# A one-core transformer block with routed experts: when the pre-split expert words are reloaded, and when the first block of rows is turned

## The chip, the cores and the metric

The kernel runs on one core of one Trainium2 chip. The metric is the device time of one execution in microseconds (us). The kernel before has a median of 651.16 us over three runs (649.86 to 651.72).

## The reference, cut to what matters

```python
x = L0_attn_x                                  # [2, 1024, 256], f32
mod = (silu(L0_c) @ L0_wmod).reshape(2, 6, 1, 256)
sa, ca, ga, sb, cb, gb = (mod[:, i] for i in range(6))       # ga, gb kept away from zero
h = layernorm(x) * (1 + ca) + sa
x = x + ga * attention(h)                      # 16 heads of 16, causal softmax, biases
h = layernorm(x) * (1 + cb) + sb
xt = h.reshape(2048, 256)
cw = combine_weights(xt, gate_w)               # 16 experts, best 2 of 4 groups, top 4, normalised
for e in range(16):
    out += cw[:, e:e+1] * (swiglu(xt @ expert_up_w[e].T) @ expert_down_w[e].T)
out += swiglu(xt @ shared_up_w.T) @ shared_down_w.T
return x + gb * out
```

The change touches only the way from the shared expert (the last line but one) to the sixteen routed experts (the loop).

## The kernel before, in words

**Stages.** Attention runs first (eight groups of heads, `attention(body)`). Behind it comes the shared expert: 20 steps in the order of `S_ORDER` (line 287), of which "u" steps make the up products of one chunk of 512 tokens and one slice of features, and "d" steps the down products; the last two, steps 18 and 19, are `("d", 3, 0)` and `("d", 3, 1)`. Last come the routed experts. The 2048 tokens times 4 choices are sorted by expert into 79 blocks (`NB`) of 128 rows, each block with a single expert; a block's expert has a number no higher than the block's. After the blocks the expert outputs are read back, scaled and summed.

**Words.** All products are made as three products of high and low parts ("split words"). An item k of the 18 (`NW`) is half of the shared expert (k = 0, 1) or one expert (k = 2 to 17). Items up to 10 are loaded raw and split on ScalarE (`high_words`) and VectorE (`low_words`) during the shared expert. Items 11 to 17 (`PRE` is 11) are split by GpSimd during attention and stored in HBM as `expert_words`; they come back, ready, by `load_final` (line 883; its transfer is issued on line 887), 1088 KB each. I call these seven transfers F11 to F17. `place_free` (line 835 on) makes a final wait until its place in SBUF is free: F11 and F12 wait among others until the last chosen rows are in HBM (line 849), F14 to F17 until the shared expert's last down products are made (`s_down`, line 842).

**The order of the transfers.** All these transfers are issued by SyncE (SP) in program order on one queue. `POST_SP` (line 241) says what SP issues after each step of the shared expert, `BLOCK_SP` (line 306) what it issues behind the rows of a block. The SP loop of the blocks is

```python
for b in range(NB):
    load_block(b)
    for piece in BLOCK_SP.get(b, ()):
        work(piece)
```

`load_block(b)` (line 952 on) reads the blocks' addresses from a small table, four at a time (line 957), and issues the load of the block's 128 rows, 132 KB, into one of four buffers `G` (line 977). I call it Gb. Before it issues, block 0 waits for all chosen rows and the pads; a block from 4 on waits for the block four before it to have been turned and its output rows found (lines 973, 974; YIX on line 1942); and

```python
if PRE <= b + NSH < NW:
    sp.wait_ge(w_raw[b + NSH], WORDS_IN)
```

with `NSH` = 2: the load of block b = 9 to 15 waits on SP until the final b + 2 has landed.

**A block on the engines.** TensorE turns its rows (`turn_unit`, lines 2362 to 2370, two transposes; tb below is the time at which block b's start), ScalarE takes the high part of the turned rows (`turn_high`, line 1418), VectorE the low part and the row numbers of the outputs (`turn_low`, lines 1929 to 1942), then TensorE makes the up products (`up_unit`, line 2415), ScalarE and VectorE the activation (lines 1424, 1968), TensorE turns it (line 2427) and makes the down products (lines 2439 to 2444), ScalarE copies the result out and GpSimd scatters it to HBM (line 1233). The turn of block s + 2 stands in TensorE's program behind the up products of block s. `turn_unit(u)` waits for Gu and for `turn_low(u - 1)`.

**At the seam.** In both engine programs `turn_unit(0)` and `turn_low(0)` stand behind step `SN - 2` = 18, so before the last step of the shared expert, whose down products (`s_down_tiles(3, 1)`, line 2335), four idle products (`idle_products`, line 2381, all at 128 x 512) and whose sum on VectorE (`s_add(3, 1)`, lines 1923 and 1927) come after them. Block 1's turn stands behind those.

Of the kernel before, what the change touches and what calls it, by code (L numbers as in the profile page):

```python
# [117 lines left out]
def interleave():  # L118
# [121 lines left out]
EARLY_LOADS = {6: (3, 4, 5), 7: (6,)}  # L240
POST_SP = {
    -1: [("store", 2), ("load", 7)], 2: [("turned", 2)], 6: [("store", 3)], 7: [("turned", 3)], 9: [("load", 8), ("load", 9)],
    11: [("pads", 0, 16)], 12: [("load", 10), ("final", 11), ("final", 12)],
}

LAST_OUT = 5
# [45 lines left out]
SN = len(S_ORDER)  # L292
# [10 lines left out]
assert all(PLACE[NSH + e] == NSH + e + sum(d for first, d in PLACE_STEPS if e >= first) for e in range(NE))  # L303
BLOCK_DVE = {1: [("lo", 10)]}

BLOCK_SP = {3: [("final", 13), ("final", 14)], 5: [("final", 15)], 6: [("final", 16)], 8: [("final", 17)]}
for _table, _lead in ((BLOCK_DVE, 5), (BLOCK_SP, 3)):
    assert all(_s <= _p[1] - _lead for _s in _table for _p in _table[_s])

# [20 lines left out]
def program(nc, x, wqk, bqk, wv, bv, wout, bout, cT, wmod, wgate, wsh, wexp, qkd, modrows, hTd, xd, padd, zd, wd, out):  # L330
    with ExitStack() as ctx:

        def sem(name):
            return ctx.enter_context(nc.semaphore(name))
# [279 lines left out]
        pads = sem("pads")  # L614
# [148 lines left out]
        def _(sp):  # L763
# [188 lines left out]
            def load_block(b):  # L952
                if b == 0:
                    sp.wait_ge(tab_ready, 1)
                if b % SP_LOAD == 0:
                    n = min(SP_LOAD, NB - b)
                    _, values = nc.values_load_multi_w_load_instructions(
                        rbt[0:1, b:b + n], engines=(mybir.EngineType.SP,), min_val=0, max_val=XROWS // P - 1,
                        skip_runtime_bounds_check_because="a block lies in its expert's stretch or behind all of them")
                    where.update({b + k: v for k, v in enumerate(values)})  # L960
                if b == 0:
                    for c in range(NC):
                        sp.wait_ge(xs_out[c], 16 * TPC * TOPK)
                    sp.wait_ge(pad_out, 16 * NE)

                    for k in range(PRE, NW):
                        sp.wait_ge(w_raw[k], WORDS_OUT)
                if b >= GRING:

                    sp.wait_ge(t1_ps, b - GRING + 1)  # L970
                    sp.wait_ge(yix_step, 2 * (b - GRING) + 2)


                sp.wait_ge(w_lo, NSH + min(b, PRE - NSH - 1) + 1)
                if PRE <= b + NSH < NW:
                    sp.wait_ge(w_raw[b + NSH], WORDS_IN)
                sp.dma_start(G[b % GRING][:, :], xd.rearrange("(n p) w -> n p w", p=P)[bass.ds(where[b], 1)].rearrange(
                    "a p w -> p (a w)")).then_inc(g_in[b % GRING], 16)

            def work(piece):  # L980
                if piece[0] == "store":
                    store_turned(piece[1])
                if piece[0] == "turned":
                    load_turned(piece[1])
                if piece[0] == "pads":
                    pad_experts(sp, mybir.EngineType.SP, piece[1], piece[2])
                if piece[0] == "load":
                    load_words(piece[1])
                if piece[0] == "final":
                    load_final(piece[1])  # L990
# [4 lines left out]
# [4 lines that stand above are left out]
# [476 lines left out]
        def _(dve):  # L1475
# [35 lines left out]
            def row_maximum(n, u):  # L1511

                i, diag, _, w = ROWS[u // HG]
                j = u % HG
                dve.wait_ge(m_ps, n * UNITS + (u + 1))
                dst = mxA[:, i, j:j + 1] if diag else mxB[:, i - TPC, j:j + 1]
                nc.vector.tensor_reduce(dst, mbank[u % RING][:, 0:w], AX.X, ALU.max).then_inc(m_red, 1)  # L1517
# [318 lines left out]
            def work(piece):  # L1836
                what = piece[0]
                if what == "res":
                    residual(piece[1], piece[2])
                if what == "stats":  # L1840
                    statistics(piece[1], piece[2])
                if what == "aggr":
                    averages(piece[1], piece[2])
                if what == "rows":
                    make_rows(piece[1], piece[2])
                if what == "soft":
                    soften(piece[1])
                if what == "ta":
                    copy_out(piece[1], piece[2])
                if what == "route":  # L1850
                    route(piece[1], piece[2], piece[3])
                if what == "norm":
                    normalise(piece[1])
                if what == "tot":
                    totals()
                if what == "tab":
                    block_tables()
                if what == "lo":
                    low_words(dve, nc.vector, piece[1])
                if what == "xl":  # L1860
                    rows_low(piece[1])
# [39 lines left out]
            def s_multiply(c, f):  # L1901
                i, n = FC * c + f, FEATS[f]
                dve.wait_ge(s_silu, i + 1)
                if i >= 2:
                    dve.wait_ge(s_low, i - 1)
                nc.vector.tensor_tensor(s_act[i % 2][0:n, :], s_up[i % 2][1][0:n, :], s_gate[i % 2][0:n, :],
                                        ALU.mult).then_inc(s_mult, 1)

            def s_rest(c, f):
                i, n = FC * c + f, FEATS[f]  # L1910
                dve.wait_ge(s_high, i + 1)
                nc.vector.tensor_tensor(s_al[i % AHR][0:n, :], s_act[i % 2][0:n, :], s_ah[i % AHR][0:n, :].bitcast(F32),
                                        ALU.subtract).then_inc(s_low, 1)

            def s_add(c, i):

                n, y = 2 * c + i, Yall[:, 2 * i:2 * i + 2, :]
                dve.wait_ge(s_down, n + 1)
                if n == 0:
                    dve.wait_ge(modrow_in, 48)  # L1920
                if n >= 2:
                    dve.wait_ge(x_add, n - 1)
                nc.vector.tensor_tensor(y, s_out[i].rearrange("p (t h) -> p t h", t=2), GBr[:, c // (S // CH), :].unsqueeze(1)
                                        .broadcast_to([P, 2, H]), ALU.mult).then_inc(s_gated, 1)
                dve.wait_ge(s_gated, n + 1)
                t = X[:, 2 * n:2 * n + 2, :]
                nc.vector.tensor_tensor(t, t, y, ALU.add).then_inc(x_add, 1)

            def turn_low(u):
                dve.wait_ge(xh_done, u + 1)  # L1930
                nc.vector.tensor_tensor(xl[u % 2][:, :], xbank[:, 0:H], xh[u % 2][:, :].bitcast(F32),  # L1931
                                        ALU.subtract).then_inc(xl_done, 1)
                find_outputs(u)
# [10 lines left out]
            for s in range(-1, SN):  # L1944
                if s >= 0 and S_ORDER[s][0] == "u":
                    s_multiply(*S_ORDER[s][1:])
                for piece in POST_DVE.get(s, ()):
                    work(piece)
                if s >= 0 and S_ORDER[s][0] == "u":
                    s_rest(*S_ORDER[s][1:])  # L1950
                if s >= 0 and S_ORDER[s][0] == "d" and not any(s in late for late in LATE_SUMS.values()):
                    s_add(*S_ORDER[s][1:])
                for d in LATE_SUMS.get(s, ()):
                    s_add(*S_ORDER[d][1:])
                for piece in POST_DVE.get(s + 0.5, ()):
                    work(piece)
                if s == SN - 2:

                    turn_low(0)

# [59 lines left out]
        def _(pe):  # L2020
# [351 lines left out]
            def idle_products(s):  # L2372

                if s < 2:
                    pe.wait_ge(s_mult, 1)
                    to = s_up[0][0]
                else:
                    was_read(pe, ("cnt",))
                    to = allb[0]
                for i in range(IDLE_PE[s]):  # L2380
                    nc.tensor.matmul(to[:, :], Wsh[:, 0:P], Wsh[:, P:P + CH], start=True, stop=True)

            for s in range(-1, SN):
                if s >= 0:
                    (s_multiply if S_ORDER[s][0] == "u" else s_down_tiles)(*S_ORDER[s][1:])
                if s in IDLE_PE:
                    idle_products(s)
                for piece in POST_PE.get(s, ()):
                    work(piece)
                if s == SN - 2:  # L2390
                    turn_unit(0)

            expert = {}
# [134 lines left out]
```

## Time and profile before

| | us |
|---|---|
| median of three runs | 651.16 (649.86 to 651.72) |
| span of the profiled execution | 644.6 |
| rest of the median that lies outside such a span | 6.6 |
| TensorE busy | 582.1 (90%) |
| VectorE busy | 487.5 (76%) |
| ScalarE busy | 382.8 (59%) |
| GpSimd busy | 337.9 (52%) |

The profiled execution has no time of its own on record beside its span; the 6.6 us is the median less the span. Times of the trace are counted from the start of the span. SPq is SyncE's own instruction stream (it issues transfers), PEld TensorE's weight load. In a row of the chain or timeline the first number is the start, the second the duration; a bracket at the end is how long the engine had been idle before the row and what ended that.

### The profile page before, as it was taken

How to read it: one execution, taken by the hardware profiler on the slowest of the kernel's cores; microseconds unless marked ns; L12 is line 12 of the kernel's file. 1: busy time of each engine (PE TensorE's matmuls, PEld its weight loads, DVE VectorE, ACT ScalarE, POOL GpSimd, SP SyncE). 2: the span in 40 equal slices, each digit the busy share in tenths (PEclk: the TensorE clock that was granted, in tenths of full speed). 3: DMA queues.
4: the chain of work that ended last, by engine and by line, in shares of the span. 5: the costliest groups of instructions: out<-in, count | busy, mean ns of one | idle time of the engine just before them, and what ended most of it. 6: DMA issues, size and time to landing. Idle time of an engine off the chain costs nothing. (4 is left out here: it accounts for less than half of the span.)

```text
span 644.6 us, 13664 instructions
## 1 busy us (share of the span) xinstructions
PE 582.1 (90%) x3960; PEld 395.7 (61%) x3960; DVE 487.5 (76%) x1415; ACT 382.8 (59%) x926; POOL 337.9 (52%) x585
## 2 busy tenths in 40 slices
PE   3879879999999999998997799997799999999996
PEld 3657533434343444444342378776799999999985
DVE  4888978888888868776967568898566766666648
ACT  3546437666766656655858552643356777776662
POOL 5524614455747527763738876774144444444430
PEclk9989969999999999998999989999799999999999
DMA  8349965961707273451305243665964444444498
GB/s 270 137 158 288 334 221 151 243 210 71 216 26 224 87 209 141 136 185 63 118 34 174 77 150 115 232 217 207 364 220 134 135 135 134 133 135 134 126 374 335
DMA packets 69066, 113.62 MB, mean 176 GB/s; under 512 B 12578, under 2 KB 51106, under 8 KB 67844
## 3 DMA queue, kind: packets, MB, share of 16 engines
q1 hardware_dynamic: 62036, 93.74, 45.3%
q0 software_dynamic: 6864, 19.01, 7.6%
q8 instruction: 34, 0.56, 0.4%
q14 instruction: 36, 0.29, 0.1%
q10 hardware_dynamic: 96, 0.01, 0.0%
HBM read 60.57 MB, written 49.94 MB: 171 GB/s over the span
## 5 line engine op out<-in xcount | busy, mean ns | idle before, releaser
L1377 ACT ACTIVATE Pr<-bank 128x512 f32<-128x512 f32 (+3 forms) x384 | 165.5, 494 | 94.8 <-PE bank L2166 91.1
L1517 DVE TENSOR_REDUCE mxA<-bank 128x1 f32<-128x128 f32 (+3 forms) x256 | 112.2, 484 | 23.9 <-PE bank L2062 23.7
L1233 POOL DMA_INDIRECT expert_rows<-Y,YIX x79 | 75.7, 959 | 104.0 <-DVE ytmp L1938 75.5
L2166 PE MATMUL bank<-Qs,Ks 99*128 99x512 bf16 (+3 forms) x384 | 118.6, 332 | 8.0 <-ACT Pr L1377 3.8
L2062 PE MATMUL bank<-Ks,Qs 96*128 96x512 bf16 (+3 forms) x384 | 122.1, 334 | 2.2 <-DVE mxA L1517 1.3
L1517 DVE TENSOR_REDUCE mxB<-bank 128x1 f32<-128x512 f32 x128 | 81.5, 681 | 13.5 <-PE bank L2062 13.4
L2152 PE MATMUL bank<-Pr,Vst 128*32 128x512 f32 (+3 forms) x768 | 83.4, 507 | 4.4 <-POOL Pr L1217 4.4
L1167 POOL DMA_INDIRECT chosen_rows<-Hx,pos x64 | 69.9, 1093 | 21.1 <-issue 17.5
L2415 PE MATMUL bank<-W,xh 128*128 x316 | 78.3, 329 | 0.4 <-issue 0.4
L1215 POOL TENSOR_TENSOR tick<-ident 128x1 f32<-128x1 f32 x128 | 25.4, 198 | 100.5 <-ACT Pr L1377 99.7
L2166 PEld LDWEIGHTS bank<-Qs,Ks 99*128 99x128 bf16 x384 | 36.0, 98 | 61.4 <-ACT Pr L1377 38.7
L2060 PE MATMUL bank<-mask,identb 128*128 128x128 bf16 x256 | 55.1, 227 | 7.7 <-DVE mxA L1517 5.3
L1968 DVE TENSOR_TENSOR act_a<-bank,sg 128x176 f32<-128x176 f32 x79 | 27.0, 342 | 45.3 <-ACT sg L1424 45.2
L2062 PEld LDWEIGHTS bank<-Ks,Qs 96*128 96x128 bf16 x384 | 38.1, 99 | 28.8 <-DVE mxA L1517 6.1
L1217 POOL TENSOR_SCALAR_AFFINE_SELECT Pr<-Pr 128x256 f32<-128x256 f32 x128 | 53.3, 416 | 0.0
L2415 PEld LDWEIGHTS bank<-W,xh 128*128 128x128 f32 x316 | 52.3, 189 | 1.3 <-issue 1.0
L2415 PE MATMUL bank<-W,xl 128*128 x158 | 51.3, 325 | 0.0
L1424 ACT ACTIVATE sg<-bank 128x176 f32<-128x176 f32 x79 | 25.1, 317 | 37.4 <-PE bank L2415 37.4
L2060 PEld LDWEIGHTS bank<-mask,identb 128*128 128x128 bf16 x256 | 25.1, 98 | 30.0 <-DVE mxA L1517 13.6
L1439 ACT ACTIVATE Y<-bank 128x256 f32<-128x256 f32 x79 | 30.3, 384 | 13.7 <-PE bank L2444 5.4
L1931 DVE TENSOR_TENSOR xl<-bank,xh 128x256 fp32r<-128x256 f32 x79 | 32.9, 416 | 5.8 <-ACT xh L1418 5.8
L2369 PE MATMUL bank<-ident,G 128*128 128x128 f32 x158 | 30.9, 278 | 6.0 <-DMA G<-chosen_rows 6.0
(254 smaller groups left out, 1314.8 us busy)
## 6 DMA issues: line engine op xcount, KB each, us to landing
G<-chosen_rows SPq DMA_DIRECT2D x79, 132.0 KB
Z<-expert_rows SPq DMA_DIRECT2D x16, 512.0 KB, 12.3
W<-expert_words SPq DMA_DIRECT2D x7, 1088.0 KB, 7.1
qk_parts<-AP SPq DMA_DIRECT2D x16, 384.0 KB, 5.0
Qs<-qk_parts SPq DMA_DIRECT2D x16, 384.0 KB, 4.2
Ks<-qk_parts SPq DMA_DIRECT2D x8, 768.0 KB, 9.0
Wraw<-in_wexp SPq DMA_DIRECT2D x9, 608.0 KB, 5.1
SA<-in_wexp SPq DMA_DIRECT2D x7, 608.0 KB, 10.5
```

What stands on the lines that cost most here:

```text
L1167: nc.gpsimd.indirect_dma_start(out=xd, out_offset=bass.IndirectOffsetOnAxis(ap=pos[:, c * TPC + t, j:j + 1], axis=0), in_=chosen(c)[:, t, ...
L1217: nc.gpsimd.affine_select(out=v, in_=v, compare_op=ALU.is_ge, fill=0.0, base=0, pattern=[[0, 2], [1, P]], channel_multiplier=-1).then_inc( ...
L1233: nc.gpsimd.indirect_dma_start(out=zd, out_offset=bass.IndirectOffsetOnAxis(ap=YIX[:, b:b + 1], axis=0), in_=Y[b % YRING], in_offset=None) ...
L1377: nc.scalar.activation(Pr[(2 * s + j // 2) % 4][:, j % 2, 0:w], ebank[p % RING][:, 0:w], ACT.Exp, scale=SCALE).then_inc(exp_done, EXP)
L1517: nc.vector.tensor_reduce(dst, mbank[u % RING][:, 0:w], AX.X, ALU.max).then_inc(m_red, 1)
L1931: nc.vector.tensor_tensor(xl[u % 2][:, :], xbank[:, 0:H], xh[u % 2][:, :].bitcast(F32), ALU.subtract).then_inc(xl_done, 1)
L2060: nc.tensor.matmul(mbank[u % RING][:, w - P:w], identb[:, :], mask[:, :], start=True, stop=False, skip_group_check=True)
L2062: nc.tensor.matmul(mbank[u % RING][:, 0:w], Qs[slot][0:NPR, i // TPC, j, (i % TPC) * P:(i % TPC + 1) * P], Ks[slot][0:NPR, j, k0:k0 + w], ...
L2152: ins = nc.tensor.matmul(pvb[32 * j:32 * j + 32, q0:CH], Vst[slot][:, kt, 32 * j:32 * j + 32], Pr[(2 * s + j // 2) % 4][:, j % 2, 0:w], st ...
L2166: nc.tensor.matmul(ebank[p % RING][:, 0:CH - q0], Ks[slot][0:NAUG, j, kt * P:(kt + 1) * P], Qs[slot][0:NAUG, qc, j, q0:CH], start=True, st ...
L2369: ins = nc.tensor.transpose(xbank[:, k * P:(k + 1) * P], G[u % GRING][:, k * P:(k + 1) * P], ident[:, :])
L2415: ins = nc.tensor.matmul(ubank[u % 2][:, 0:2 * EI], x_part[u % 2][:, k * P:(k + 1) * P], words(u, first + k * 2 * EI, 2 * EI), start=(k == ...
```

## The change

It does three things. The finals are issued behind other block loads: F11 and F12 no longer after step 12 of the shared expert, so ahead of G0, but behind G4 and G6; F13 and F14 behind G8 and G10 instead of G3; F15 behind G12 instead of G5; F16 behind G13 instead of G6; F17 behind G14 instead of G8. `turn_low(0)` on VectorE and `turn_unit(0)` on TensorE move from behind step 18 to behind step 19.

```diff
@@ -240,7 +240,7 @@
 EARLY_LOADS = {6: (3, 4, 5), 7: (6,)}
 POST_SP = {
     -1: [("store", 2), ("load", 7)], 2: [("turned", 2)], 6: [("store", 3)], 7: [("turned", 3)], 9: [("load", 8), ("load", 9)],
-    11: [("pads", 0, 16)], 12: [("load", 10), ("final", 11), ("final", 12)],
+    11: [("pads", 0, 16)], 12: [("load", 10)],
 }
@@ -303,7 +303,8 @@
 BLOCK_DVE = {1: [("lo", 10)]}
 
-BLOCK_SP = {3: [("final", 13), ("final", 14)], 5: [("final", 15)], 6: [("final", 16)], 8: [("final", 17)]}
+BLOCK_SP = {4: [("final", 11)], 6: [("final", 12)], 8: [("final", 13)], 10: [("final", 14)], 12: [("final", 15)], 13: [("final", 16)],
+            14: [("final", 17)]}
 for _table, _lead in ((BLOCK_DVE, 5), (BLOCK_SP, 3)):
     assert all(_s <= _p[1] - _lead for _s in _table for _p in _table[_s])
@@ -1954,7 +1955,7 @@
                 for piece in POST_DVE.get(s + 0.5, ()):
                     work(piece)
-                if s == SN - 2:
+                if s == SN - 1:
 
                     turn_low(0)
 
@@ -2387,7 +2388,7 @@
                     idle_products(s)
                 for piece in POST_PE.get(s, ()):
                     work(piece)
-                if s == SN - 2:
+                if s == SN - 1:
                     turn_unit(0)
```

## Rows read from the trace of the kernel before

**Rows 1.** The page: span, and the 40 slices for clock and DMA.

```profile
span 644.6 us, 13664 instructions
...
PEclk9989969999999999998999989999799999999999
DMA  8349965961707273451305243665964444444498
```

**Rows 2.** The chain that ended last, in order of time, around the seam.

```profile
443.18 2.49 DMA chosen_rows<-Hx,pos
445.81 0.33 SPq L887
446.31 0.32 SPq L887
446.68 0.32 SPq L957
447.56 6.25 DMA G<-chosen_rows
...
462.38 7.57 DMA G<-chosen_rows
```

**Rows 3.** Timeline of SP: two finals in one row, then a block's load and a final.

```profile
449.58 6.60 SPq L887 DMA_DIRECT2D W<-expert_words  x2
...
460.84 0.33 SPq L977 DMA_DIRECT2D G<-chosen_rows  x1
461.27 0.39 SPq L887 DMA_DIRECT2D W<-expert_words  x1
```

**Rows 4.** DMA issues with us to landing: F11, F14, F15 alone; the 128 KB stores.

```profile
W<-expert_words SPq DMA_DIRECT2D x1, 1088.0 KB, 4.9
...
W<-expert_words SPq DMA_DIRECT2D x1, 1088.0 KB, 6.6
...
W<-expert_words SPq DMA_DIRECT2D x1, 1088.0 KB, 5.9
...
out<-X SPq DMA_DIRECT2D x2, 128.0 KB, 1.7
```

**Rows 5.** Timeline of TensorE: the seam, and the turns of blocks 0, 1, 4, 8, 15.

```profile
448.83 0.28 PE L2335 MATMUL bank<-W,s_al 96*128 96x256 f32 x1
453.85 0.69 PE L2369 MATMUL bank<-ident,G 128*128 128x128 f32 x2 [4.75 <-DMA G<-chosen_rows]
...
455.62 1.91 PE L2381 MATMUL bank<-W 128*128 128x512 f32 x4
457.32 0.63 PE L2369 MATMUL bank<-ident,G 128*128 128x128 f32 x2
...
462.85 0.44 PE L2369 MATMUL bank<-ident,G 128*128 128x128 f32 x2 [0.70 <-DMA G<-chosen_rows]
...
472.10 0.38 PE L2369 MATMUL bank<-ident,G 128*128 128x128 f32 x2
...
486.67 0.38 PE L2369 MATMUL bank<-ident,G 128*128 128x128 f32 x2
```

**Rows 6.** Timeline of VectorE: the sum of step 18, and block 8's row numbers.

```profile
450.12 0.69 DVE L1927 TENSOR_TENSOR X<-X,Y 128x512 f32<-128x512 f32 x1
...
473.71 0.16 DVE L1942 TENSOR_REDUCE YIX<-ytmp 128x1 uint32<-128x4 f32 x1
```

**Rows 7.** Timeline of SP: the issue of G12.

```profile
474.06 0.33 SPq L977 DMA_DIRECT2D G<-chosen_rows  x1
```

**Rows 8.** Busy time by stretch: engines, TensorE's granted clock, DMA share, GB/s.

```profile
449.00:451.50 2.50, 0.11 (x1) 0.00 (x0) 1.77 (x3) 0.12 (x1) 0.00 (x0) 1.00 1.00 418
...
454.00:458.40 4.40, 4.40 (x17) 3.90 (x18) 2.10 (x5) 0.77 (x2) 0.00 (x0) 0.51 0.92 344
...
480.00:500.00 20.00, 20.00 (x151) 19.78 (x150) 13.98 (x61) 12.56 (x41) 9.58 (x10) 1.00 0.45 135
```

**Rows 9.** The table of block addresses: when it is written.

```profile
L1815 DVE CAST rbt<-bank x1: 222/222/222, 436.6 to 436.6; 1x80 int32<-1x80 f32 x1
```

## The prediction

> **What bounds the kernel now.** I read the page first [rows 1]: TensorE is busy nearly everywhere, its clock is high, and one slice of the DMA line stands at nine tenths where the shared expert hands over to the blocks. Then the chain of waits [rows 2]: up to 445.67 us it hangs on the last chosen rows reaching HBM, then on two finals that SP issues ahead of the first block's rows, then for 6.25 us on those rows. The timeline of TensorE shows the price [rows 5]: its last product before the hole starts at 448.83, and the turn of block 0 starts at 453.85 after 4.75 us of idleness. While it waits the DMA engines are busy throughout, at 418 GB/s [rows 8]. Behind the hole the clock is at the lower level, 0.51 of full on average from 454.0 to 458.4 [rows 8]. Later come two small waits for rows behind other finals, 0.70 us at block 4's turn [rows 5] and one at block 7's at the end of the 7.57 us transfer [rows 2]. After that the stage is bound by TensorE: from t8 = 472.10 to t15 = 486.67 seven blocks take 14.57 us, 2.08 us each [rows 5], and TensorE is busy 20.00 of 20 us [rows 8].
>
> **The change, part by part.**
>
> *G0 without finals ahead of it.* SP is released at 445.67 to 445.81 [rows 2]. The address table was written at 436.6 [rows 9], so its reading (line 957, at 446.68 before) now lies ahead of that wait. G0 is issued at about 445.9 instead of 447.56. For the landing of 132 KB I take 2.0 us; the nearest row is the 128 KB store with 1.7 [rows 4], and the upper end is G0's own 6.25 behind two finals. It lands at about 447.9, and nothing needs it yet.
>
> *The turn behind the last products.* TensorE goes straight on from 448.83 + 0.12. The six products of the second half take about 0.8, the four idle ones at the full clock half of their 1.91 [rows 5], so 0.95; then t0 is about 450.7. VectorE ends the sum of step 18 at 450.81 [rows 6] and now does that of step 19 ahead of `turn_low(0)`: two instructions of 0.69, to about 452.2, and the low part of block 0 by 452.6. This is the later of the two, so t1 = 452.65 against 457.32 [rows 5]: 4.67 us earlier. The moved turn itself costs nothing, being covered by that sum; without the cover it would cost the way over ScalarE and VectorE, at most the 1.4 us of the sum.
>
> *Blocks 1 to 8.* Before, t4 - t1 = 5.53 with 0.70 of waiting, so 4.83 without. Between t4 and t8 lay 9.25 us [rows 5]; undisturbed, four blocks at 2.05 (between the 2.00 that I count in a full stretch and the 2.08 above) take 8.2. Do F11 and F12 disturb them? G4 is issued at about t0 + 2.5, F11 0.43 behind it [rows 3], and G5 and G6 queue behind F11. F11 took 4.9 us to land [rows 4], so by about 458.5; block 5 is wanted at 459.5, block 7, behind F12, at 463.6, with F12 landed by 462. Slack of 1 us or more everywhere: no stall. So t8 is about 452.65 + 4.83 + 8.2 = 465.7, which is 6.4 us ahead. Were it all, the change would bring 6.4 us.
>
> *Blocks 12 to 15.* Here a new wait appears. SP issues block b's rows only when the final b + 2 has landed, and that final now stands directly behind the rows of block b - 1 for b = 13, 14 and 15, and behind the rows of block b - 2 for b = 12. SP is one stream and waits at each: G12, F15, wait for it, G13, F16, wait, G14, F17, wait, G15. One turn of this chain is p = 0.43 from the issue of rows to that of the final [rows 3], plus the final's landing, plus 0.19 from release to issue (YIX ends at 473.87, G12 is issued at 474.06 [rows 6, 7]). The landing is bounded below by F11's 4.9, alone on the queue and without scatters, and above by F14's 6.6, which still had F13 ahead of it [rows 4]. A block's own rows and scatter hold the DMA engines for 0.45 of 2.0 us, 0.9 us [rows 8], part of which falls into each final's flight, so I take the middle, 5.4. Hence p = 6.0, with ends of 5.5 and 7.2.
>
> Without the new waits, the rows of block b are issued 1.96 us after t(b - 4) (474.06 less 472.10 [rows 7, 5]). So G10 goes out at t6 + 2.0 = 461.6 + 2.0 = 463.6, F14 behind it. G12 then waits for F14, G13 to G15 for one final each: four turns, and G15 is issued at 463.6 + 4p and usable 2.0 later. t15 = 465.6 + 4p, against 486.67. With p = 6.0 that is 489.6, **2.9 us later than before**; the ends of p give 1.0 and 7.7 later. The lead of 6.4 us is eaten: TensorE waits about 2 us at block 13 and 4 us at each of blocks 14 and 15. Queued behind the waiting SP instruction are only the later row loads; VectorE, ScalarE and GpSimd stand idle with TensorE. Block 16's rows go out 0.5 us behind G15 and are no longer late, and from there the stage runs as before.
>
> The Trainium skill puts a price on a final (DMA: Bandwidth & Descriptors, "Anatomy of one DMA"): 2.0 us plus the bytes at 436 GB/s, an estimate of 4.6 for 1088 KB. F11 with 4.9 stands near it, F14 and F15 far off, and the measurement decides; by that estimate p would be 5.2, and the sum about zero.
>
> *The clock.* Two waits of 4 us with 2 us of work between them lie just under the 4.75 us after which the clock was at its lower level until 458.4 [rows 5, 8]. In the waits that costs nothing, as the slower work ends before the next rows land; behind block 15 it does. Upper bound: 4.4 us of work at half the clock, 2.2 us lost; lower: none. I take 0.9. The clock loss at the old hole is already in t1.
>
> The Trainium skill speaks against the change here (TensorE: Matmul & The Clock Gate, "HAM oscillation"): bursts of products shorter than the DMA waits between them run at half clock, each anew. By that the upper bound would hold and the sum be 5.1.
>
> *Edits at nothing:* SP's other transfers keep their order, POOL's and ACT's programs are untouched; F13's landing (issued with G8) meets G11 just in time.
>
> **Sum.** +2.9 + 0.9 = +3.8 on the profiled span, 644.6 to 648.4; the median lies 6.6 above that span, and I carry the difference over: 651.2 + 3.8 = 655.0. A measurement of this kernel can tell about 0.3%, 2.0 us, from no change.
>
> **The rivals.**
> - *Short landings* (no change). Finals land in 4.9 with little traffic, since the stalled blocks send little themselves; p = 5.5 or below, no clock loss: +1.0 or less, 651 to 652. For it: F11. Against it: no other final came in under 5.9, and each of the four follows a row load on the same queue. Chance 0.17. (The Trainium skill's figure above would put it here.)
> - *The lead outlasts the chain* (faster). Its place is the same four waits; it decides at p = 5.27, where 4p = 21.07, and clears 2.0 us only below 4.77. If p stayed at or under the pace of the blocks the whole 6.4 would remain, 644.8. Against it: 4.77 leaves 4.15 for a landing, less than any row has. Something would have to be wrong in my reading of SP's order. Chance 0.06.
> - *Heavy landings and cold clock* (slower still, inside the forecast's side): p = 6.6 and 2.2 of clock, +7.5, 658.7. Chance 0.12.
> - *The change does not do what it says*: G0 is held by the pads or by item 10's load, both issued before 434, 12 us earlier. Then t1 stays and only the chain's cost is left, well over 658. Chance 0.01.
> - The forecast itself, +2 to +6: 0.64.
>
> **How the numbers follow.** Slower by over 0.3%: 0.64 + 0.12 + 0.01 = 0.77; within: 0.17; faster: 0.06. The range takes the low landings from +0.6 and the heavy ones to +7.5: 651.8 to 658.7.
>
> **What would show it.** G0 issued near 446 and no wait of TensorE at 449; t1 near 452.7; t8 near 465.7; seven finals issued one by one, the last four about 6 us apart; SP waiting on finals; TensorE waiting for rows three times between 475 and 490 for 2, 4 and 4 us; t15 near 489.6; a dip of the clock there. It is wrong if the finals land in under 4.8 us, if SP shows no waits for them, or if t8 is not ahead by about 6.

## The result, and the profile after

| | before | changed |
|---|---|---|
| median of the runs | 650.51 us (649.14 to 651.72, 4 runs) | 659.37 us (657.59 to 661.04, 4 runs) |
| span of the profiled execution | 644.6 us | 658.1 us |

The ratio is 1.0133, with a 95% interval of 1.0107 to 1.016: 8.7 us slower, between 7.0 and 10.4. The direction was forecast, the size was not: the forecast was 3.8 us, and its range ended at 658.7, 0.7 below the median measured.

The page of the changed kernel first (span, granted clock, DMA in 40 slices):

```profile
span 658.1 us, 13664 instructions
...
PEclk9979969999999999996977889999988999999999
DMA  8359957863616352551114143673965444444498
```

The spans differ by 13.5 us, more than the medians, and the clock line shows lower digits in the middle, in the attention, where the change has no instruction. So the two executions cannot be laid over each other from the start. I therefore count from a fixed point close to the change, A: the start of TensorE's first product with the last slice of features in step 18, 448.13 us before and 454.26 here. I call the time from A to the turn of block 15 **the seam**; it was 38.5 us and is now 46.0, 7.4 more. From block 15's turn to the end it is 157.9 us in both. The remaining 6.1 us of the 13.5 lie ahead of A.

The timeline of SyncE (SP), where line 978 is now the load of a block's rows and line 888 that of a final:

```profile
452.12 7.34 SPq L978 DMA_DIRECT2D G<-chosen_rows  x5
459.64 0.33 SPq L888 DMA_DIRECT2D W<-expert_words  x1
...
471.52 0.49 SPq L888 DMA_DIRECT2D W<-expert_words  x1
475.88 4.46 SPq L978 DMA_DIRECT2D G<-chosen_rows  x2
480.44 0.40 SPq L888 DMA_DIRECT2D W<-expert_words  x1
```

The timeline of TensorE, the turns of blocks 0, 1, 5, 13, 14 and 15 (they answer to [rows 5]):

```profile
456.72 0.38 PE L2370 MATMUL bank<-ident,G 128*128 128x128 f32 x2
458.74 0.41 PE L2370 MATMUL bank<-ident,G 128*128 128x128 f32 x2 [1.64 <-DVE xl L1932]
...
466.69 0.44 PE L2370 MATMUL bank<-ident,G 128*128 128x128 f32 x2 [0.20 <-DMA G<-chosen_rows]
...
488.39 0.44 PE L2370 MATMUL bank<-ident,G 128*128 128x128 f32 x2 [3.40 <-DMA G<-chosen_rows]
...
494.86 0.44 PE L2370 MATMUL bank<-ident,G 128*128 128x128 f32 x2 [2.63 <-DMA G<-chosen_rows]
...
500.22 0.44 PE L2370 MATMUL bank<-ident,G 128*128 128x128 f32 x2 [1.89 <-DMA G<-chosen_rows]
```

The hole of 4.75 us at block 0 [rows 5] is gone, and three waits for rows stand at blocks 13 to 15. The chain that ended last, in order of time, names their cause (it answers to [rows 2]):

```profile
460.55 6.09 DMA G<-chosen_rows
...
471.52 8.27 DMA W<-expert_words
...
480.44 5.55 DMA W<-expert_words
...
486.64 5.54 DMA W<-expert_words
...
492.85 5.06 DMA W<-expert_words
...
498.12 2.05 DMA G<-chosen_rows
```

Four finals, F14 to F17, one after the other, and G15 behind them. And SP's own waits in the stretch from 440 to 520 us:

```profile
SPq L975 <- DVE YIX L1943: 22.7, 15, 4.6
SPq L977 <- DMA W<-expert_words: 21.0, 5, 5.1
```

21.0 us in five waits for finals; in the kernel before SP had none of them. The first of the five is for F13, ahead of the rows of block 11, which was still turned without a wait of TensorE. Lastly the busy times of four stretches (PE, PEld, DVE, ACT, POOL, then granted clock, DMA share, GB/s):

```profile
452.00:459.00 7.00, 4.35 (x31) 3.62 (x29) 6.12 (x12) 2.74 (x5) 0.00 (x0) 1.00 0.31 77
459.00:472.00 13.00, 12.07 (x81) 10.80 (x80) 9.41 (x37) 6.78 (x21) 2.88 (x3) 1.00 0.86 291
472.00:480.00 8.00, 6.78 (x49) 6.29 (x48) 4.58 (x20) 4.08 (x13) 2.88 (x3) 1.00 0.86 321
480.00:500.00 20.00, 12.30 (x67) 11.01 (x65) 7.85 (x34) 6.26 (x19) 4.79 (x5) 0.83 0.68 228
```

The DMA engines are now little used (0.31) at the very place where they ran full before [rows 8], and busy (0.86) from 459 on, when the blocks bring their own traffic.

### The profile page after: what moved, and what is told of

Read it like the earlier page. It is cut to its first block and busy times, and to the rows that moved or that the text cites. A ratio compares the mean times of both kernels' runs of the same rounds, so it can differ in the third digit from the quotient of the medians.

```text
span 658.1 us, 13664 instructions
## 1 busy us (share of the span) xinstructions
PE 593.6 (90%) x3960; PEld 399.7 (61%) x3960; DVE 488.2 (74%) x1415; ACT 383.5 (58%) x926; POOL 339.9 (52%) x585
## 5 line engine op out<-in xcount | busy, mean ns | idle before, releaser
L2167 PE MATMUL bank<-Qs,Ks 99*128 99x512 bf16 (+3 forms) x384 | 122.2, 345 | 6.0 <-DMA Qs<-MT 3.0
L2063 PE MATMUL bank<-Ks,Qs 96*128 96x512 bf16 (+3 forms) x384 | 123.6, 338 | 2.0 <-DVE mxA L1518 1.3
L1518 DVE TENSOR_REDUCE mxB<-bank 128x1 f32<-128x512 f32 x128 | 81.5, 681 | 13.5 <-PE bank L2063 13.4
L2153 PE MATMUL bank<-Pr,Vst 128*32 128x512 f32 (+3 forms) x768 | 86.4, 524 | 5.5 <-POOL Pr L1218 5.5
L1168 POOL DMA_INDIRECT chosen_rows<-Hx,pos x64 | 71.7, 1120 | 21.4 <-issue 17.5
L2167 PEld LDWEIGHTS bank<-Qs,Ks 99*128 99x128 bf16 x384 | 36.6, 100 | 62.4 <-ACT Pr L1378 38.2
L2061 PEld LDWEIGHTS bank<-mask,identb 128*128 128x128 bf16 x256 | 25.4, 100 | 30.1 <-DVE mxA L1518 13.3
```

Of the source, the lines that this page charges most:

```text
L1168: nc.gpsimd.indirect_dma_start(out=xd, out_offset=bass.IndirectOffsetOnAxis(ap=pos[:, c * TPC + t, j:j + 1], axis=0), in_=chosen(c)[:, t, ...
L2061: nc.tensor.matmul(mbank[u % RING][:, w - P:w], identb[:, :], mask[:, :], start=True, stop=False, skip_group_check=True)
L2063: nc.tensor.matmul(mbank[u % RING][:, 0:w], Qs[slot][0:NPR, i // TPC, j, (i % TPC) * P:(i % TPC + 1) * P], Ks[slot][0:NPR, j, k0:k0 + w], ...
L2153: ins = nc.tensor.matmul(pvb[32 * j:32 * j + 32, q0:CH], Vst[slot][:, kt, 32 * j:32 * j + 32], Pr[(2 * s + j // 2) % 4][:, j % 2, 0:w], st ...
L2167: nc.tensor.matmul(ebank[p % RING][:, 0:CH - q0], Ks[slot][0:NAUG, j, kt * P:(kt + 1) * P], Qs[slot][0:NAUG, qc, j, q0:CH], start=True, st ...
```

## The experiments

The runs come from five groups on several chips, each with the kernel before beside it; its medians there were 650.5 to 665.5 us. So times are compared only as ratios to the kernel before of the same group. The seam is compared across groups, with one reservation that the second control below shows. All times after a "+" are counted from A.

| run | ratio to before (95%) | block 1's turn | block 8's | seam |
|---|---|---|---|---|
| before, first profile | | +9.2 | +24.0 | 38.5 |
| before, control | 0.9974 (0.9927 to 1.0021) | +3.2 | +19.1 | 33.4 |
| changed, first | 1.0133 (1.0107 to 1.016) | +4.5 | +18.8 | 46.0 |
| changed, control | 1.0218 (1.0152 to 1.0285) | +4.5 | +18.8 | 46.6 |
| e1 turns only | 1.002 (0.9984 to 1.0055) | +5.9 | +22.1 | 37.3 |
| e2 finals only | 1.0179 (1.0101 to 1.0256) | +3.2 | +17.5 | 46.0 |
| e3 F15 to F17 a block earlier | 1.0131 (1.0051 to 1.0211) | +4.5 | +20.2 | 42.0 |
| e4 wait on TensorE | 1.0039 (0.9998 to 1.0081) | +4.5 | +18.7 | 38.3 |
| e5 finals on ScalarE's queue | 1.0055 (1.0016 to 1.0094) | +4.6 | +25.1 | 39.2 |
| e6 F11 and F12 in the lull | 1.0121 (1.0078 to 1.0165) | +4.5 | +20.3 | 45.4 |
| e7 rows first | 1.0003 (0.9973 to 1.0034) | +3.2 | +25.4 | 39.6 |
| e8 late finals only | 1.0207 (1.0156 to 1.0259) | +9.3 | +23.9 | 51.1 |
| e9 spread, wait on TensorE | 0.9932 (0.9901 to 0.9964) | +3.2 | +20.5 | 34.6 |
| e10 spread, wait on SP | 0.9955 (0.992 to 0.9989) | +3.2 | +18.4 | 34.9 |

**The two halves of the change (e1, e2).** e1 is the kernel before with only this, in two places:

```diff
-                if s == SN - 2:
+                if s == SN - 1:
```

> Only the turns of block 0 are moved behind step 19; the finals stay as before. My theory (the lead at the seam comes from G0 no longer queueing behind two finals): the hole before block 0's turn stays, only the ten products that now run inside it are saved, block 1's turn comes 1 to 2 us earlier, no chain of waits behind it: 0.5 to 2 us under before, about 649.5. Rival (the moved turns are what costs, since VectorE's sum now stands ahead of the low part): 1 us or more above before.

Measured: no difference within the interval, so neither the gain of 0.5 to 2 us nor a cost of 1 is confirmed. Block 1's turn is at +5.9 and the seam at 37.3, but SP was also released earlier, 3.7 us ahead of A instead of 2.3, so I count from the issue of F11. Block 1's turn stands 9.5 us behind it, against 11.5 before, as expected; block 15's stands 40.9 us behind it in both. The gain is there at block 1 and gone by block 15. e2 is the changed kernel with these two lines put back.

> Only the finals are moved as in the changed kernel; the turns stay behind step 18. My theory (the loss is SP's chain of waits for finals, which starts at block 10's load): as slow as the changed kernel within 1 us, 658.5 to 659.5, with the same three waits at blocks 13 to 15. Rival (turns cost): several us faster than the changed kernel.

The seam is that of the changed kernel to a tenth. With the turns back, block 1 is turned 1.3 us sooner (+3.2 against +4.5), so behind early rows the moved turn costs 1.3. That gain too is gone by block 15: G10 goes out 1.4 us sooner (+15.4 against +16.8), but from there to the issue of G15 it takes 28.3 us instead of 27.1. The ratio, 1.0179, has the changed kernel's 1.0133 in its interval. The loss is the finals'.

**The chain of waits (e3, e4).** e3 takes the changed kernel with

```diff
-BLOCK_SP = {4: [("final", 11)], 6: [("final", 12)], 8: [("final", 13)], 10: [("final", 14)], 12: [("final", 15)], 13: [("final", 16)],
-            14: [("final", 17)]}
+BLOCK_SP = {4: [("final", 11)], 6: [("final", 12)], 8: [("final", 13)], 10: [("final", 14)], 11: [("final", 15)], 12: [("final", 16)],
+            13: [("final", 17)]}
```

> The changed kernel with F15, F16 and F17 each issued one block earlier (behind the rows of blocks 11, 12 and 13), so that a final is in flight while SP waits for the one before. Theory (serial latency: one final at a time, issue to landing, nothing overlapped): the turn of the chain falls from about 6 to the 4.1 us that a final takes when it streams behind another, three times, so block 15's turn and the end come 5 to 6 us earlier, about 653.5. Rival (the DMA engines are full, the order of the waits is indifferent): no change against the changed kernel, 659.

G12 to G15 are issued at +27.7, 31.9, 36.6 and 39.9: 4.1 us apart on the mean, where the changed kernel has 6.0. The seam is 3.9 to 4.5 us shorter than in the two profiles of the changed kernel, less than the 5 to 6 expected: the three turns save 5.9, but block 8 is turned 1.4 us later and the way from G10 to G12 takes 9.6 us instead of 9.0. So finals that overlap pass faster than one at a time, and the DMA engines, with a share of 0.68 from 480 to 500 in the changed kernel, had the room. (The ratio, on its own chip, is too wide to show it.)

e4 leaves every transfer where the changed kernel has it and moves the wait:

```diff
@@ load_block
-                if PRE <= b + NSH < NW:
-                    sp.wait_ge(w_raw[b + NSH], WORDS_IN)
@@ up_unit
                 pe.wait_ge(xl_done, u + 1)
+                if PRE <= u + NSH < NW:
+                    pe.wait_ge(w_raw[u + NSH], WORDS_IN)
```

> The changed kernel, but block b = 9 to 15 waits for its final on TensorE ahead of its up products, not on SP ahead of its rows. Theory (SP's wait for a final delays the rows behind it, which have nothing to do with it): the three waits of 3 to 4 us at blocks 13 to 15 shrink to 0 to 2 us, since rows queue behind finals only in the transfer; 7 to 9 us under the changed kernel, about 651. Rival (the finals' landing itself is what the blocks need): the wait moves to TensorE's up products and little is gained, 657 to 659.

The seam falls from 46.0 to 38.3, by 7.7, as expected, and the time to 1.0039 of before. TensorE's waits in its stretch from 450 to 520 us:

```profile
PE bank L2368 <- DMA G<-chosen_rows: 3.1, 2, 2.2
```

No wait for a final is among them: the blocks did not need the finals so soon. It was SP's wait, and the rows queued behind it, that stopped them.

**Finals on a queue of their own (e5).** The kernel of e4 with an empty `BLOCK_SP`, and on ScalarE, behind its last step of the shared expert,

```diff
+            for k in range(PRE, NW):
+                load_final_act(k)
```

where `load_final_act` is `load_final` with its waits and its transfer on ScalarE.

> All seven finals are issued on ScalarE's own queue, one behind the other, at the end of the shared expert; blocks 9 to 15 wait for them on TensorE; G0 first and the turns as in the changed kernel. By the seam I mean the time from TensorE's first product with the last slice of step 18 (448.13 before, 454.26 in the changed kernel) to block 15's turn: 38.5 us before, 46.0 changed, 38.3 with the wait on TensorE alone. Theory (rows queued behind finals, and SP waiting for finals, are the whole loss): the seam is 33 to 35 us, 4 to 5 under before, ratio to before about 0.993. Rival (the DMA engines are simply full, 11 MB in that stretch): 38 us, no gain over before. A third way it could go: the seven finals land later than blocks 9 to 15 want them, the wait shows at the up products.

This theory fell. TensorE still waited for rows, at block 4 (second row, 3.76 us), and the turns up to block 7 came late:

```profile
480.54 0.41 PE L2389 MATMUL bank<-ident,G 128*128 128x128 f32 x2
...
486.14 0.44 PE L2389 MATMUL bank<-ident,G 128*128 128x128 f32 x2 [3.76 <-DMA G<-chosen_rows]
...
489.76 0.49 PE L2389 MATMUL bank<-ident,G 128*128 128x128 f32 x2
```

The first of the later row loads is G4, issued by SP at 477.54:

```profile
477.54 22.43 SPq L975 DMA_DIRECT2D G<-chosen_rows  x9
```

With nothing ahead of it on SP's queue it was usable 8.6 us later. A second queue did not shield this small transfer from the large ones. The third way did not come about: from block 8 to block 15 the turns are 2.0 us apart, with no wait for a final.

**Where the finals stand (e6, e8).** e6 takes the changed kernel with

```diff
-BLOCK_SP = {4: [("final", 11)], 6: [("final", 12)], 8: [("final", 13)], 10: [("final", 14)], 12: [("final", 15)], 13: [("final", 16)],
+BLOCK_SP = {3: [("final", 11), ("final", 12)], 6: [("final", 13)], 8: [("final", 14)], 12: [("final", 15)], 13: [("final", 16)],
```

> The changed kernel with F11 and F12 behind G3 (where its DMA engines lie idle for 2.4 us), F13 behind G6, F14 behind G8; F15 to F17 stay behind G12, G13, G14. Theory (F13 and F14 took 8 us to land because four finals were issued every 4 us beside the blocks' own traffic, which asks for more than 4 us of the DMA engines; F15 to F17 are slow for being waited for one at a time): SP no longer waits for F13 and F14, G12 goes out 2.0 us after block 8's turn, the three turns of 6 us stay, the seam is 40 to 42 against 46.0. Rival (a final takes 8 us whenever blocks run): F13 and F14 still land after 8 us, seam 44 or more.

The seam, 45.4 us, is where the rival put it. Its chain:

```profile
481.79 8.11 DMA W<-expert_words
...
490.63 7.79 DMA W<-expert_words
...
499.07 5.77 DMA W<-expert_words
...
505.50 4.86 DMA W<-expert_words
...
510.58 2.12 DMA G<-chosen_rows
```

F14 took 8.11 us although F11 and F12 were long in. F15 was alone: it was issued at 490.63, after F14's landing at 489.90, and still took 7.79. So no backlog of finals is needed for nearly 8 us. F16 and F17, with stalled blocks around them, took 5 to 6.

But the rival's reason, "a final takes 8 us whenever blocks run", does not hold. Four finals beside running blocks: F11 of the changed kernel, F16 of e9, and F14 and F15 of the changed kernel's control (these two from its chain):

```profile
W<-expert_words SPq DMA_DIRECT2D x1, 1088.0 KB, 5.0
...
W<-expert_words SPq DMA_DIRECT2D x1, 1088.0 KB, 5.6
...
490.34 9.16 DMA W<-expert_words
...
500.15 5.02 DMA W<-expert_words
```

TensorE was busy for the whole flight of F11, F16 and the control's F15. So beside running blocks a final took anything from 5.0 us to 9.2 (9.8 in e2), and being beside running or stalled blocks does not settle its length. What does repeat is the place: F14 took 8.1 to 9.8 us in the five profiles in which it is issued behind G8 or G10 and SP waits for it (changed, control, e2, e6, e8), and in the four of them that have the changed kernel's order from G10 on, the three finals behind it took 4.9 to 6.0. What makes F14 slow there was not found.

e8 is the kernel before with the changed places for F13 to F17 alone:

```diff
-BLOCK_SP = {3: [("final", 13), ("final", 14)], 5: [("final", 15)], 6: [("final", 16)], 8: [("final", 17)]}
+BLOCK_SP = {8: [("final", 13)], 10: [("final", 14)], 12: [("final", 15)], 13: [("final", 16)], 14: [("final", 17)]}
```

> The kernel before with F13 to F17 issued where the changed kernel issues them (behind G8, G10, G12, G13, G14), F11 and F12 and the turns as before. Theory (SP's chain of waits is the whole loss; the first of its turns was long only since F11 and F12 were still in the queue): F13 and F14 land in 5.5 to 6.5 us instead of 8, and from G10 on four turns of 6 us follow: block 15's turn 26 us behind the issue of G10, slower than before by 5 to 9 us, by 0.8 to 1.3%. Rival (F14's 8.3 us is what a final takes beside running blocks): the first turn is 8 to 9 us again.

```profile
473.11 8.29 DMA W<-expert_words
...
482.05 5.99 DMA W<-expert_words
...
488.69 5.00 DMA W<-expert_words
...
494.35 5.14 DMA W<-expert_words
```

Again F14 takes 8.3 and the first turn of the chain 9.0 (G10 at 472.65, G12 at 481.62), so the rival was right about this turn. Block 15's turn is 29.2 us behind the issue of G10, not 26, and G15 is issued 27.1 us behind G10, as in the changed kernel (471.06 to 498.12). The seam is 12.5 us longer than in the first profile of before, the time 2.07% longer (13.5 us of 651), outside the 5 to 9 us expected. The late finals alone cost more than the whole change; putting the rows first gives part of it back.

**The controls, and rows first (e7).**

> The changed kernel again, on the chip of the other runs of this call, as their control. Both theories: seam 46.0 us within 0.5, ratio to before about 1.013. If the part ahead of the seam differs from that of the kernel before in its profile, that part scatters between executions.

> The kernel before again, as a control: ratio 1.000, seam 38.5 us within 0.5, and behind block 15's turn 158 us. The part ahead of the seam shows how far it scatters without any change.

The changed kernel nearly repeats: its seam is 46.6, 0.6 us longer, with F14 at 9.2 us, but its ratio of 1.0218 lies above the 1.013 expected. The kernel before does not repeat: 33.4 against 38.5. Its SP and TensorE timelines, where F11 and F12 are issued, at the last slice of step 18, and at the turns of blocks 0 and 1:

```profile
461.68 0.83 SPq L887 DMA_DIRECT2D W<-expert_words  x2
```

```profile
468.72 0.50 PE L2335 MATMUL bank<-W,s_ah 96*128 96x256 f32 x2
...
469.69 0.44 PE L2369 MATMUL bank<-ident,G 128*128 128x128 f32 x2
...
471.88 0.41 PE L2369 MATMUL bank<-ident,G 128*128 128x128 f32 x2
```

Block 0's turn stands 8.0 us behind the issue of F11, exactly as in the first profile (453.85 less 445.81); but the release came 7.0 us ahead of A here and 2.3 there. The hole at block 0 exists only where the chosen rows are late against TensorE, as in the profile from which I predicted. The same reading fits e1 (F11 3.7 us ahead of A, block 0's turn at +4.4) and e8, whose program is that of before up to there: released 2.3 us ahead of A, it has the hole again, 4.82 us. Over all fourteen profiles the release stands 2.1 to 2.3 us ahead of A in six and 3.7 to 10.3 in the others, so neither kind is rare among them. The changed kernel does not feel the difference at block 1: released 2.1 and 10.3 us ahead, it turns it at +4.5 both times. Ahead of A this execution took 468.7 us and not 448.1, with no change in the kernel at all.

e7 is the kernel before with

```diff
-    11: [("pads", 0, 16)], 12: [("load", 10), ("final", 11), ("final", 12)],
+    11: [("pads", 0, 16)], 12: [("load", 10)],
-BLOCK_SP = {3: [("final", 13), ("final", 14)], 5: [("final", 15)], 6: [("final", 16)], 8: [("final", 17)]}
+BLOCK_SP = {3: [("final", 11), ("final", 12), ("final", 13), ("final", 14)], 5: [("final", 15)], 6: [("final", 16)], 8: [("final", 17)]}
```

> The kernel before with one edit: F11 and F12 go behind G3 (so G0 to G3 ahead of them), F13 and F14 directly behind those; turns and later finals as before. It asks whether the hole at block 0's turn was a cost. Theory A (the hole was 4.7 us of cost, as I predicted): block 0's turn comes right behind the last products and the seam (first product of the last slice of step 18 to block 15's turn) is 3 to 5 us shorter than in the kernel before at the same release of SP. Theory B, formed from the control of the kernel before (block 0's turn stood 8.0 us behind SP's release in three executions, block 4's 17): G4 stands behind the same four finals, so block 4's turn stays about 17 us behind the release and the time is within 1 us of before; the ratio is 1.000.

Theory B holds. Blocks 0 and 1 are turned at +0.8 and +3.2, the hole is gone, and the ratio is 1.0003: block 4 waits 6.4 us instead, and its turn at +14.6 is 16.8 us behind SP's release (-2.1), nearly as in before (462.85 less 445.81, 17.0). A hole closed at block 0 that only moves to block 4 gains nothing.

**A version that beats both (e9, e10).** Both issue F11 and F12 behind G3, F13 behind G4, F14 behind G6, F15 behind G8, F16 behind G10 and F17 behind G11, with block 0's turns as before; e9 has the wait on TensorE.

> A version that could beat both: G0 to G3 first, F11 and F12 behind G3, F13 behind G4, F14 behind G6, F15 behind G8, F16 behind G10, F17 behind G11; blocks 9 to 15 wait for their final on TensorE; turns as before. Theory (no wait of SP, small queue ahead of each block's rows): seam 34 to 37, against 38.5 and 33.4 in the two executions of the kernel before; ratio 0.995 to 1.002. Rival (the DMA engines carry 11 MB in this stretch in any order, so no order helps): ratio 1.000 to 1.005.

```profile
SPq L975 <- DVE YIX L1941: 44.0, 30, 2.9
SPq L968 <- DMA chosen_rows<-Hx,pos: 7.9, 1, 7.9
```

SP waits for the blocks and never for a final, TensorE waits for rows once (1.5 us), and the time is 0.68% under before (0.36 to 0.99). The seam, 34.6 us, is 3.9 shorter than in the first profile of before and 1.2 longer than in its control; in this profile the release stands 2.1 us ahead of A, so the first (2.3) is the nearer comparison. e10 is the same order with the wait left on SP, so a change of tables alone:

> The order of the faster version (F11 and F12 behind G3, F13 behind G4, F14 behind G6, F15 behind G8, F16 behind G10, F17 behind G11) in the kernel before, with its turns and with the wait for the finals left on SP. Theory (what counts is that each final has landed when SP comes to the block that needs it; in the run with the wait on TensorE all seven had): SP waits under 1 us for finals, seam 34 to 36, ratio to before 0.992 to 0.998, like the version with the wait on TensorE. Rival (the gain came from moving the wait to TensorE): SP waits for finals again, ratio 0.998 or above.

```profile
SPq L977 <- DMA W<-expert_words: 3.2, 1, 3.2
```

One wait for a final, more than the 1 us expected, and a seam of 34.9: 0.45% under before (0.11 to 0.8). The interval reaches the rival's 0.998, so the time alone does not rule the rival out. But the intervals of e9 and e10 overlap, so where the wait stands is not shown to matter once the order is right.

## Why the prediction was right in kind and wrong in size

*G0 without finals ahead; the turns.* Right for the profiled execution: block 1's turn was predicted at 452.65, which is +4.52, and is at +4.48 in both profiles of the changed kernel. What was wrong was to take that execution for all. In the control of before, where the rows are released early, block 1's turn is at +3.2, so the lead of 4.7 us is a loss of 1.3. Nor does the median lie 6.6 us above a span: the changed kernel's profiled run took 659.87 us for its 658.1, 1.8 more. If the same holds before, its profiled execution was some 4 us faster than its median; carrying the 6.6 over did not change the difference that was forecast.

*Blocks 1 to 8.* "Slack of 1 us or more everywhere: no stall" failed by 1.2 us: block 8 is at +18.8, not +17.6. G5, behind F11, took 6.09 us, and block 5 was turned 3.04 us behind block 4.

*Blocks 12 to 15.* The mechanism and its place were right: SP's four waits, TensorE idle at blocks 13, 14 and 15, and e4 takes 7.7 us away with that wait alone. The term that was mis-sized, and with it the step that failed, is p, 6.0 us for all four turns, and in it the landing, taken as 5.4 us: F14's took 8.27. Issue to issue the turns were 8.95 (G10 at 471.06 to G12 at 480.01), 6.20, 6.20 and 5.71. The last three are within 0.3 of it; the first is 2.95 over, above the 7.2 I had called the upper end. I had bounded a landing by F14's 6.6 [rows 4] in the kernel before, though the page's view there has a median of 7.1 for the seven finals, and the last two, F16 and F17, took 8.1 and 7.9, F17 with F16 in flight for its first 3.8 us. The changed kernel's F14 had F13 in flight for its first 3.8 us. F16's 8.1 would have put the first turn at 8.7. I had let the blocks' traffic count once, as 0.9 us.

What makes F14's landing 8.3 us stays open. A sum made behind the result fits it: alone, F11 took 4.9; 1.114 MB (1088 KB) at the 418 GB/s of the full queue [rows 8] are 2.7 of it, 2.2 are left as fixed. From 472 to 480 us all queues together moved 321 GB/s; running blocks ask for 135 of these [rows 8], 186 are left, and 1.114 MB take 6.0 us, with the 2.2 about 8.2. But 321 is no ceiling: in e9, where F17 took 6.7 us beside blocks at full pace, all queues moved 412.

```profile
474.00:478.00 4.00, 4.00 (x32) 3.96 (x32) 3.24 (x17) 2.52 (x8) 1.92 (x2) 1.00 1.02 412
```

Nor does the sum give the 5.0 of F11 in the changed kernel or the 7.8 of F15 in e6, during which all queues moved only 219 GB/s. Nor is it settled by whether the blocks run: F15 of the changed kernel took 5.55 with TensorE busy for 4.55 of it, and F15 of its control 5.02 with TensorE busy throughout. What the runs show is the place: in the changed kernel, its control, e2 and e8 F14 took 8.3 to 9.8, the three finals behind it 4.9 to 6.0.

The price that the prediction quotes from the Trainium skill (DMA: Bandwidth & Descriptors, "Anatomy of one DMA") is given there as a fit for the path through GpSimd, while SyncE issues the finals. F11 with 4.9 in the kernel before and F17 with 5.06 in the changed one lie near its 4.6; F14 with 8.27 does not.

*The sum.* From A, block 15's turn was predicted at +41.5 and is at +46.0. The 4.5 are 1.3 (G10 later), 2.95 (first turn), 0.1 (the other three) and 0.1 (G15's landing, 2.1).

*The clock.* It fell (0.59 from 488 to 492, 0.93 and 0.63 behind), but gave no 0.9 us, the other term that was wrong: from block 15's turn to the end it is 157.91 against 157.92 (158.1 in the control of before, 158.4 in that of the changed kernel). By the Trainium skill's rule (TensorE: Matmul & The Clock Gate, "HAM oscillation") each burst would have paid; the slow clock was there, but inside the waits. In e2 and e6, where the low stretch reached past block 15, the tail was 159.1 and 159.3, so 1.2 to 1.4 us.

*From 7.4 to 8.7.* The profile's seam explains 7.4 of 8.7 (7.0 to 10.4). The rest would be filled if typical executions of before had a shorter seam than the profiled one; in the control pair the seams differ by 13.1 and the times by 2.18% of 665, 14.5. How often each kind of execution occurs was not measured, so this part of the cause is argued and not shown.

*The rivals.* "The lead outlasts the chain" and "short landings" needed p at or under 5.5 for all four turns; no run with this order of finals had that. The rival on the forecast's own side, heavy landings, was nearest: +7.5, at a chance of 0.12.

## What to carry to other kernels

A semaphore wait in the stream that issues transfers stops every transfer behind it; put it at the engine that uses the data, or issue the awaited transfer early enough that it has landed when the stream comes there. Price a prefetch beside running work by the longest landings that the trace shows in like company (8.1 us stood in the profile before the change, 8.3 came), not by its landing time on an idle queue (4.9). When a hole is closed in front of a full queue, look for the next transfer that stands behind the same bytes: here it moved from block 0 to block 4 and gained nothing. And take the hole from more than one profile: this one was absent in the second.

## What the runs showed of the hardware that was not expected

- A 132 KB load on its own queue, beside 1088 KB loads on another engine's queue, was usable 8.6 us after its issue (e5), and 2.05 us behind an idle queue (G15 in the changed kernel).
- A 1088 KB load landed after 4.9 to 5.1 us where it was the first on an idle queue, and after 4.9 to 9.8 beside the traffic of blocks. With no other such load in flight and TensorE busy nearly throughout it took 7.79 once (F15 in e6) and 5.02 once (F15 in the control of the changed kernel). What sets it was not found.
- The same kernel reached the same instruction at 448.1 us in one execution and at 468.7 in another, in another group of runs; the part behind block 15's turn differed by 0.2 (157.92 and 158.12).
